# Flamingo layer, fold at the start: values folded straight to keys on the partitions, 13 of 77 keys by transposes, one mixed order of value and key units

## What is computed

```python
x = x + tanh(g_xattn[0]) * xattn(layernorm(x), ctx_768, Wq, Wk, Wv, Wo, bo)   # softmax over 77 keys, 16 heads
x = x + tanh(g_ffn[0]) * (layernorm(x) @ W[idx] + b[idx])                     # idx = argmax(log_softmax(logits) - log(-log(u)))
```

## Time and profile before

| | us |
|---|---|
| median of 3 runs (1070.23 to 1073.98) | 1071.11 |
| the profiled execution | 1072.84 |
| its span, first to last instruction | 1070.8 |
| PE busy in it | 1049.6 |
| DVE busy in it | 931.8 |
| mean granted clock of PE | 0.998 |

### The profile page before, as it was taken

How to read it: one execution, slowest core, us unless ns; L and a number is a source line. 1 busy time by engine, 2 the same in 40 slices (tenths; PEclk the granted TensorE clock), 3 DMA queues, 4 the chain that set the end, 5 groups by cost and what they waited for, 6 DMA issues and landing times.

```text
span 1070.8 us, 16059 instructions
## 1 busy us (share of the span) xinstructions
PE 1049.6 (98%) x5369; PEld 531.6 (50%) x5369; DVE 931.8 (87%) x1397; ACT 347.6 (32%) x549; POOL 304.6 (28%) x444
## 2 busy tenths in 40 slices
PE   8888999999999999999999999999999999999998
PEld 6554444444554455544554455444554455445443
DVE  4878798899888988899889988899889988898895
ACT  3685332223232323223222323223222323232331
POOL 0663422212222222212222222212221222222221
PEclk9999999999999999999999999999999999999999
DMA  8799555555555454545555454545454554545453
GB/s 308 158 186 177 128 114 109 118 109 112 114 111 120 100 124 104 125 102 119 108 117 113 108 118 107 127 96 125 105 120 106 114 113 112 117 103 123 105 99 93
DMA packets 366602, 130.30 MB, mean 122 GB/s; under 512 B 345152, under 2 KB 346228, under 8 KB 366580
## 3 DMA queue, kind: packets, MB, share of 16 engines
q1 hardware_dynamic: 366084, 129.22, 56.0%
q10 hardware_dynamic: 432, 0.79, 0.4%
q0 software_dynamic: 64, 0.00, 0.0%
HBM read 27.21 MB, written 16.78 MB: 41 GB/s over the span
## 4 chain that ended last, share of the span: by engine, by line
PE 87%; DMA 4%; DVE 4%; SPq 3%; ACT 1%; POOL 1%; issue 1%; DVEq 0%; ACTq 0%
PE banks L1092 82%; SPq L440 3%; PE banks L1297 3%; DMA late<-late 2%; PE banks L1131 1%; DVE red L807 1%; DMA pick_area<-in_L_ffn_u 1%; PE banks L1198 1%; DVE late L376 1%; DMA vw_area<-last_slot 0%; DMA last_slot<-late 0%; POOL last_slot L565 0%; DVE last_slot L1019 0%; DVE fold_area L883 0%; DVE early L836 0%
## 5 line engine op out<-in xcount | busy, mean ns | idle before, releaser
L1092 PE MATMUL banks<-fold_area,early 128*128 128x462 f16 (+1 forms) x2304 | 410.6, 336 | 0.3 <-DMA early<-early 0.3
L1092 PE MATMUL banks<-vw_area,late 128*128 128x512 f16 x1701 | 379.1, 380 | 5.6 <-DMA late<-late 5.6
L1092 PEld LDWEIGHTS banks<-fold_area,early 128*128 128x128 f16 x2304 | 224.0, 97 | 187.6 <-DMA early<-early 0.8
L1092 PEld LDWEIGHTS banks<-vw_area,late 128*128 128x128 f16 x1701 | 166.4, 98 | 198.5 <-issue 6.7
L605 POOL TENSOR_TENSOR stats<-stats,cst 128x1 f32<-128x1 f32 x64 | 12.1, 189 | 650.1 <-DVE stats L1034 650.1
L973 DVE TENSOR_REDUCE stats<-banks 128x6 f32<-128x462 f32 (+1 forms) x192 | 111.6, 581 | 81.1 <-PE banks L1092 81.1
L1092 PE MATMUL banks<-late,last_slot 128*128 128x512 f16 x744 | 170.7, 379 | 0.4 <-DMA last_slot<-late 0.4
L783 ACT ACTIVATE late<-late 128x1232 f16<-128x1232 f32 (+1 forms) x66 | 79.1, 1199 | 208.1 <-DVE late L992 207.8
L733 ACT ACTIVATE late<-last_slot 128x512 f16<-128x512 f32 x64 | 40.3, 630 | 325.9 <-DVE last_slot L1046 325.9
L769 ACT ACTIVATE late<-late,cst 128x462 f32<-128x462 f32 (+1 forms) x192 | 120.7, 629 | 56.1 <-DVE late L979 56.1
L1092 PEld LDWEIGHTS banks<-late,last_slot 128*128 128x128 f16 x744 | 72.2, 97 | 89.0 <-DMA last_slot<-late 1.4
(11 more groups left out here) (115 smaller groups left out, 689.3 us busy)
## 6 DMA issues: line engine op xcount, KB each, us to landing
out<-last_slot SPq DMA_DIRECT2D x64, 256.0 KB, 2.2
early<-in_x SPq DMA_DIRECT2D x61, 256.0 KB, 2.7
fold_area<-in_L_xattn_Wo SPq DMA_DIRECT2D x4, 512.0 KB, 10.0
vw_area<-in_L_xattn_Wq SPq DMA_DIRECT2D x2, 1024.0 KB, 10.9
vw_area<-in_L_xattn_Wk SPq DMA_DIRECT2D x2, 768.0 KB, 12.4
late<-late SPq DMA_TRANSPOSE x66, 4.9
vw_area<-in_L_ffn_W SPq DMA_DIRECT2D x1, 1024.0 KB, 7.8
early<-early SPq DMA_TRANSPOSE x64, 3.1
```

Of the source, the lines that this page charges most:

```text
L1092: mm = nc.tensor.matmul(ps, lhs(l), rhs(r), start=first and n == 0, stop=last and n == 2)
```

## The change

Value units give the keys on the partitions directly. For a batch and a group of four heads (two pairs of heads; `FOURS` = 4), four matmuls of 64 contraction rows and 64 output rows write the first 64 keys of four heads, each with all 512 output columns: the row half is the head's half of the pair, the column half (partitions 0 to 63 or 64 to 127) is the pair. There are 16 such units of 1024 elements for each partition. The other 13 keys of each head (`REST`) are folded as before, transposed: four "remainders", one for each 128 output columns, with 16 matmuls of 52 columns (4 batches x 13). ACT copies their 832 elements in two instructions, POOL splits them, and one DMA transpose of 2048 columns for each turns them: 4 in place of 16.

One list, `VISITS`, gives the order to all engines. Four PSUM pairs are visited in the old ring order. The first projection now stands before the spread of Wo. Four of 16 value units are staged (5, 8, 11, 14). The query copies move from ACT to DVE. All transposing of Wq is done before the first key unit, which waits for it. From value unit 10 on there are four key units to one value unit, and eight key units at the end. Since the memory is laid out anew, FFN weights are loaded once. On SP the loads of x for batches 1 to 3 (ACT issued them before) stand behind the last value unit, around the transpose of x for tile 0; `bias` follows.

Probabilities are laid out to match: for each of 16 heads 64 keys in chunks 0 to 7, then 16 times 13 in chunks 8 and 9. ACT's high part and DVE's low part are two instructions each (1024 and 208 elements), and `EARLY` becomes 6.

```diff
+    CORE = DH
+    REST = J - CORE
+    MAIN = HEADS * CORE // P
...
-        EARLY = BANKS[1][1] * J // P
+        EARLY = BANKS[1][1] * CORE // P
...
-        STAGED_VALUES = [0, 2, 4]
+        STAGED_VALUES = [5, 8, 11, 14]
         STAGED_KEYS = [1, 5]
-        PROJECTED_AFTER = [7, 10, 13]
-        SPREAD_AFTER = 17
-        TURNED_AFTER = 22
-        KEYS_TURNED_AFTER = [1, 5, 9]
...
+        PROJECT, REMAINDER, VALUE, SPREAD, TURN, KEY = range(6)
+        VISITS = [(PROJECT, 0), (PROJECT, 1), (REMAINDER, 0), (VALUE, 0), (REMAINDER, 1), (VALUE, 1), (PROJECT, 2), (REMAINDER, 2),
+                  (VALUE, 2), (REMAINDER, 3), (VALUE, 3), (PROJECT, 3), (VALUE, 4), (VALUE, 5), (SPREAD, 0), (VALUE, 6), (TURN, 0),
+                  (VALUE, 7), (TURN, 1), (VALUE, 8), (TURN, 2), (VALUE, 9), (TURN, 3)]
+        for n in range(10, VALUES):
+            VISITS += [(KEY, 4 * (n - 10) + m) for m in range(4)] + [(VALUE, n)]
+        VISITS += [(KEY, v) for v in range(UNITS - HP, UNITS)]
+
+        def pair_of(kind, n=0):
+            return ROUND[place_of(kind, n) % len(ROUND)]
...
-            return ([KT - 1, 0][v % 2], v // 2) if v < 2 * HP else (v // HP - 1, v % HP)
...
+            return (v // HP + 1) % KT, v % HP
...
-            for t in range(KT - 1):
-                turn_values(t)
-            sp.wait_ge(vwT_done, 2 * UNITS)
...
+            sp.wait_ge(pads_set, 1)
+            for t in range(KT):
+                sp.wait_ge(side_lo, 4 * (t + 1))
+                sp.dma_start_transpose(vw_side[:, t].rearrange("p b c n -> p (b c) n"),
+                                       sides[:, t].rearrange("p b n -> p (b n)")).then_inc(side_turned, 16)
+            sp.wait_ge(v_folded, 4 * VALUES)
+            sp.dma_start(xin[:, 1, :], x[1, 0:P, :]).then_inc(x_loaded[1], 16)
...
             turn_x(0, 0)
-            turn_values(KT - 1, 0, B // 2)
+            for r in range(2, B):
+                sp.dma_start(xin[:, r, :], x[r, 0:P, :]).then_inc(x_loaded[r], 16)
             turn_x(0, 1)
-            sp.wait_ge(vw_turned[KT - 1], 16 * B // 2)
+            sp.wait_ge(v_stage_lo, len(STAGED_VALUES))
...
+            def side_split(t):
+
+                value, side = side_stage[t % 2], sides[:, t]
+                pool.wait_ge(side_staged, 2 * (t + 1))
+                nc.gpsimd.tensor_copy(side[:, :, 0:P + TAIL], value).then_inc(side_hi, 1)
+                pool.wait_ge(side_hi, t + 1)
+                nc.gpsimd.tensor_tensor(side[:, :, 2 * P:3 * P], value[:, :, 0:P], side[:, :, 0:P], ALU.subtract).then_inc(side_lo, 1)
...
+            copy_k(0)
...
-                nc.scalar.activation(ps[:, h0 * J:h1 * J], probs[:, h0 * J:h1 * J], ACT.Copy,
+                values = by_head(probs[:, h0 * J:h1 * J])
+                nc.scalar.activation(by_core(ps[:, h0 * CORE:h1 * CORE]), values[:, :, 0:CORE], ACT.Copy,
+                                     scale=2.0 ** PROB_BITS).then_inc(p_hi, 1)
+                nc.scalar.activation(by_rest(ps[:, MAIN * P + h0 * REST:MAIN * P + h1 * REST]), values[:, :, CORE:J], ACT.Copy,
...
+            def copy_q(n):
+
+                first = pair_of(TURN, n)
+                dve.wait_ge(wqT_done, 2 * n + 2)
+                dve.wait_ge(scale_q_ready, 1)
+                nc.vector.tensor_scalar(wqT[:, 2 * n:2 * n + 2, :], banks[:, first:first + 2, :], scale_q, None, ALU.mult).then_inc(wqT_copied, 1)
+
...
-                    low(ps[:, LOW + h0 * J:LOW + h1 * J], probs[:, h0 * J:h1 * J], 2.0 ** PROB_BITS,
-                        ps[:, h0 * J:h1 * J]).then_inc(p_lo, 1)
+                    values = by_head(probs[:, h0 * J:h1 * J])
+                    hi, lo = ps[:, 0:LOW], ps[:, LOW:2 * LOW]
+                    dve.wait_ge(p_hi, 2 * pieces_done(q, b, piece))
+                    cols = slice(h0 * CORE, h1 * CORE)
+                    low(by_core(lo[:, cols]), values[:, :, 0:CORE], 2.0 ** PROB_BITS, by_core(hi[:, cols])).then_inc(p_lo, 1)
+                    cols = slice(MAIN * P + h0 * REST, MAIN * P + h1 * REST)
+                    low(by_rest(lo[:, cols]), values[:, :, CORE:J], 2.0 ** PROB_BITS, by_rest(hi[:, cols])).then_inc(p_lo, 1)
...
+            def remainder(t):
+
+                first = pair_of(REMAINDER, t)
+                for h in range(HP):
+                    for e in range(2):
+                        rows = slice(DH * e, DH * e + DH)
+                        place = banks[:, first + e, 0:B * HP * REST].rearrange("p (b h j) -> p b h j", b=B, h=HP)[:, :, h, :]
+                        last_keys = vT[rows, h, :].rearrange("p (b j) -> p b j", b=B)[:, :, CORE:J]
+                        mm = nc.tensor.matmul(place, wo_raw[rows, h, t * P:(t + 1) * P], last_keys, start=True, stop=True)
+                        if h == HP - 1:
+                            mm.then_inc(side_done, 1)
+
+            def value_unit(n):
+
+                b, four = n // FOURS, n % FOURS
+                first = pair_of(VALUE, n)
+                for a in range(2):
+                    for e in range(2):
+                        rows, h = slice(DH * e, DH * e + DH), 2 * four + a
+                        nc.tensor.matmul(banks[CORE * a:CORE * (a + 1), first + e, :], vT[rows, h, b * J:b * J + CORE], wo_raw[rows, h, :],
+                                         start=True, stop=True).then_inc(v_folded, 1)
+
+            def key_fold(v):
+
+                k, h = key_unit(v)
                 for e in range(2):
                     rows = slice(DH * e, DH * e + DH)
+                    nc.tensor.matmul(banks[:, pair_of(KEY, v) + e, 0:BJ], wqT[rows, h, k * P:(k + 1) * P], kT[rows, h, :],
+                                     start=True, stop=True).then_inc(a_done, 1)
...
+            for place, (kind, n) in enumerate(VISITS):
+                taken_before(place)
+                if kind == PROJECT:
+                    keys_of(2 * n)
+                    keys_of(2 * n + 1)
+                if (kind, n) == (PROJECT, 0):
+                    pe.wait_ge(v_copied, 2)
+                    spread(WO, 2)
+                    spread(VV, 3)
...
-                taken = max(v for v in range(UNITS) if key_bank(v) == n // 2 * 2)
-                needed = LAST_TURN + -(-BANKS[n][1] // 2) - 1
+                taken = max(v for v in range(UNITS) if pair_of(KEY, v) == n // 2 * 2)
+                needed = UNITS - HP + (3, 5, 7)[n]
```

More of the change, by code:

```diff
@@ L343, in key_staged, with place_of, staged, staged_before @@
+        assert sorted(n for kind, n in VISITS if kind == KEY) == list(range(UNITS))
+        def place_of(kind, n=0):
+            return VISITS.index((kind, n))
+        def pair_of(kind, n=0):
+            return ROUND[place_of(kind, n) % len(ROUND)]
+        def key_unit(v):
+            return (v // HP + 1) % KT, v % HP
+        def staged(n):
+            return n in STAGED_VALUES
+        def staged_before(n):
+            return sum(m < n for m in STAGED_VALUES)
         def key_staged(v):
@@ L579, in _ @@
-            for n in range(staged_before(UNITS)):
-                staged_value(n)
-                if n == 7:
+                nc.gpsimd.tensor_tensor(pair_of_heads(k, 1, h), value, pair_of_heads(k, 0, h), ALU.subtract).then_inc(k_stage_lo, 1)
+            for kind, n in VISITS:
+                if kind == REMAINDER:
+                    side_split(n)
+                if kind == VALUE and staged(n):
+                    value_split(n)
+                if kind == KEY and key_staged(n):
+                    key_split(n)
+                if (kind, n) == (VALUE, 8):
@@ L582, in _ @@
                     x_scale(0, 0)
-            for n in range(key_staged_before(UNITS)):
-                staged_key(n)
-                if n == 1:
+                if (kind, n) == (KEY, 26):
                     x_scale(0, 1)
@@ L701, in _, with side_copied @@
-            act.dma_start(xin[:, 1, :], x[1, 0:P, :]).then_inc(x_loaded[1], 16)
-            for v in range(UNITS):
+            def side_copied(t):
+                act.wait_ge(side_done, 2 * (t + 1))
+                if t >= 2:
+                    act.wait_ge(side_lo, 4 * (t - 1))
+                for e in range(2):
+                    place = side_stage[t % 2].rearrange("p b (i e m) -> p b i e m", i=FOURS, e=2)[:, :, :, e, :]
+                    value = banks[:, pair_of(REMAINDER, t) + e, 0:B * HP * REST].rearrange("p (b i m) -> p b i m", b=B, i=FOURS)
+                    nc.scalar.copy(place, value).then_inc(side_staged, 1)
@@ new lines, in value_high @@
+            def value_high(n):
+                first = pair_of(VALUE, n)
+                act.wait_ge(v_folded, 4 * (n + 1))
+                if staged(n):
+                    m = staged_before(n)
+                    if m == 1:
+                        act.wait_ge(side_lo, 4 * KT)
+                    if m >= 2:
+                        act.wait_ge(v_stage_lo, m - 1)
+                    nc.scalar.copy(v_stage[m % 2], banks[:, first:first + 2, :]).then_inc(v_staged, 1)
+                else:
+                    if n >= VALUES - FOURS:
```

(32 more changed lines are left out.)

504 lines of the change are left out of this document (186 added, 318 removed).

## The result

The changed kernel took 1081.45 us (median of 6 runs, 1078.44 to 1083.81) against 1072.38 for the kernel before on the same chip: a ratio of 1.0084, 95% interval 1.0063 to 1.0106, so 9.1 us slower, where +4.7 was forecast. That is outside the forecast's own range (1074.4 to 1079) and inside the stated one (1066.0 to 1083.0). The profiled execution took 1080.38 with a span of 1078.4.

The account below looks back on a forecast made before the run. PE bounds the tiles, so the fold's start moves everything: 7.8 later first scores, minus 2.1 and 1.7 won before and in tile 0's attention, plus 0.7 for splits, +4.7: 1075.8 us median, range 1066.0 to 1083.0 (own 1074.4 to 1079).

Parts of the forecast that it names:

- The start: Fold up to the last projection: PE-bound, scaling of vT 2.9 us late at 28.5, projections ending at 48.75.
- Rival 3: Value units: the four 64x64 matmuls run as two pairs, 0.86 longer each; +13.2, 1084.3 us; chance 0.08.
- The middle: From the last projection on, DVE works without a gap; first key unit on PE at 63.25, for 61 before.
- The mixed groups: Four key units and a value: hand-over through bank pairs costs 4.36 us, not 3.3; two groups with one staged value 8.1.
- S: Start of the first scores on PE: forecast 95.7 for 87.86 before, 7.8 us late.
- The wait for the last key unit: Ahead of the first scores: the last key unit shares their bank pair, so they wait for DVE's very last low half.
- A: Start of the attention of tile 0: forecast 15.45 behind the first scores for 17.58 before, 2.1 us won.
- From A to the end: Attention of tile 0 onward: full clock wins 1.7 us, split probabilities lose 0.7, nothing lost in steady tiles.
- loss of 0.25 in each of three tiles: Three tiles without slack ahead of PE: the split probabilities cost 0.25 each, 0.7 us lost.
- Rival 4: Steady tiles: the probability split breaks the 0.74 us slack; about 1084 us at 0.9; chance 0.03.
- Rival 1: Fold: DVE's 13.3 us idle stays, with about 50 of work from 29.8; +2.1, 1073.2 us, no change; chance 0.28.
- Rival 2: Fold: the drain becomes the bound and the hand-over hides; first scores at 86, -5, 1066.1 us, faster; chance 0.19.

Follow-up runs that it names:

- a: Changed kernel with the spread of Wo again ahead of the projection of keys; ratio 1.0073 to the kernel before.
- g: Changed kernel with value unit 5 not staged through POOL, DVE taking its low parts; ratio 1.0067 to the kernel before.
- c: Changed kernel with the four scaled query copies back on ACT; ratio 1.0074 to the kernel before.
- e: Changed kernel with small PE transposes filling two gaps, 16 ahead of the first key unit and 14 ahead of the first scores; ratio 1.0061 to the kernel before.
- b: Changed kernel with the ring of bank pairs turned, so the last key unit avoids the first scores' banks; ratio 1.0045 to the kernel before.
- i: Changed kernel with a to d together and tile 0's high and low parts of x three key units later; 1069.78 us for 1072.87 before.
- j: Version i with value unit 5 also not staged through POOL; 1067.46 us for 1073.20 of the kernel before.
- h: Changed kernel with the split of each group's 64-key probabilities doubled on ACT and DVE; ratio 1.0096 to the kernel before.
- d: Changed kernel with value units 10 to 15 ahead of all key units; ratio 1.0036 to the kernel before.

## Why the prediction was right in direction and short by half

**The start held.** Scaling of vT was forecast at 28.5 and stood at 28.26; a value unit 1.0, measured 1.02; a remainder 1.85, measured 1.93; the end of the last projection 48.75, measured 48.66. Rival 3 is refuted by the records. PE idled 1.72 ahead of the second spread. The sum contained that wait, as it put the spread at 27.15 (measured 26.91) and the next projection at 27.45 (27.07); what it didn't say is that the wait could be had back (a).

**The middle was short by 1.6**, of which 1.3 is the product of the scales (1.72 for the 0.40 that the 2.3 of the powers contained). Value 5's staging on POOL was booked at no cost, since it is buffered; its cost is that DVE waits for it. The net cost is smaller: without the staging DVE has a low half more, and the first key unit gains 0.43 (g). The DVE prices taken from the rows held: 1024 elements 1.19 to 1.23, a query copy 1.28, following at 1.19.

**The mixed groups were right, their first one was not.** From value 12 to 13 DVE's low halves lie 4.28 apart (79.05, 83.33), forecast 4.36; from 13 to 15, with a staged one, 7.99 (91.32), forecast 8.1. But from the first key unit to the end of value 10 (PE's restart behind its low half, 72.34) I had 6.05 and the trace has 7.5. In versions a, c, e and g, at full clock, it is 7.15 to 7.2, so the lower clock adds 0.3. The 1.1 that is left I put down to the normalization of x for tile 0, which stands in no sum of mine: DVE does it between those key units (0.87 at 65.96 in the trace of g), ACT stands 1.08 until it has it, and the next key units' high parts come behind. No run takes it out alone. The last eight key units took 6.3 for 5.8, which wasn't followed. Together S came 3.25 later than forecast: 1.6 + 1.1 + 0.3 + 0.5, less 0.25 in the groups.

**The wait for the last key unit was right and incomplete.** The forecast had the first scores behind DVE's very last low half because of the bank pair, and b shows it. It didn't follow the gap to its second price: PE stands 2.79 us, and the scores then run at the lower clock, 1.7 us (e). The prediction said that this loss would vanish, as the gap ahead of attention shrinks; that came true there (attention 5.99), and the same 1.7 came back in the scores. Here a step of the sum failed: a won clock was booked without asking where the new gap lies. A stood 16.95 behind S for 15.45, the difference being this. It is 1.5 us of the miss; the 3.25 of S, most of it the product of the scales and the normalization of x, is the larger part.

**From A to the end** the forecast had 1.7 won and 0.7 lost; the profiled executions have 2.9 won. 1.66 is the attention's clock; 0.7 are waits of PE, which come to 4.1 before and 3.4 in the changed trace; two of before, 0.37 at 173.67 and 0.29 at 198.09, have one of 0.18 in their place. The rest is spread and wasn't followed. The forecast loss of 0.25 in each of three tiles doesn't show: PE idles 0.29 ahead of the last scores in both. So the profiled spans differ by only 7.6 us, the medians by 9.1. The six executions of the changed kernel say where to look for the difference: 1078.44 us with a mean clock of 1.000, 1079.26 and 1080.38 with 0.997, 1082.52 and 1082.78 with 0.995, 1083.81 with 0.994. The slower ones had more of the lower clock than the profiled one (1080.38); in which stretch, no trace shows.

**Luck in the total.** In the spans the forecast missed S by 3.25 and the way from S to A by 1.5, both too early, and the rest by 1.9 the other way (2.9 won for 1.0). The direction rests on what was shown, the late start and the mixed order; that +4.7 came as near as it did owes something to errors of opposite sign. And 1081.45 is nearer to the 1084 of rivals 3 and 4, which the traces refute, than to the forecast's 1075.8.

**Rivals.** Rival 1 took the waste as fixed. Busy time by windows, sum of 26.85 to 98.95 us of the changed kernel (columns as in the earlier trace rows):

```profile
sum 72.10, PE 60.46 PEld 33.08 DVE 56.23 ACT 43.44 POOL 43.70; mean PE 30.23 PEld 16.54 DVE 28.12 ACT 21.72 POOL 21.85
```

DVE worked 56.2 of 72.1 us and stood 15.9, for 13.3 before. From 29.80, where rival 1 begins its sum, it worked 53.9 and stood 15.2, for the 50 and 13.3 of that rival: it fails by the work (3.9) more than by the waste (1.9). Rival 2 (the hand-over hides) wasn't what this change does, but it is what the fold does once the order is another: i and j have PE's streams of key units with gaps of 0.3 to 0.6 and S at 67.4 and 66.0 from T0, where the rival's 86 would be 64.2. Rival 4 is refuted: the change leaves 0.55 of the slack of 0.74, and even the doubled split 0.39.

## What to carry to other kernels

A change that touches the order of a start-up brings small waits of its own (here 1.9, 2.8, 2.8 and 4.6 us of the first scores for a spread, a bank pair, an engine and a mixed order); undone one at a time they tell what each is worth, and here the three behind the start nearly added up when undone together, to a kernel faster than both. The first did not: it waits for two engines, and which of them is last changes from execution to execution. In a ring of buffers, mixing two kinds of units can make each hand-over cost its full latency (here 4.28 us a group for 3.3 of work); runs of one kind, the one that the next stage doesn't wait for first, let it hide. When a gap of an engine whose clock falls moves, move its clock loss with it in the sum: fill the gap or place it before work that something else bounds.

## What the runs showed of the hardware that was not expected

- DVE's product of two scales, one element a partition, took 1.71 to 1.73 us in all eight versions that stage value 5 (the change, a to e, h, i), each time begun inside POOL's subtraction of 2.12 to 2.13 that reads SBUF and ended with it, and 0.16 without it (g, j). Before, it took 0.40 and ended at 51.14, as POOL's copy of 0.70 from 50.42 did. The reciprocal at 53.15, with one input of one element, ran in 0.16 beside the same subtraction. The Trainium skill (SBUF — State Buffer, section SBUF: two separate sides) says that a VectorE instruction with two inputs in SBUF and a GpSimd instruction that reads SBUF exclude each other for the whole instruction. The trace agrees: the product has two inputs in SBUF. That a form with one input would go through at this place was not tried.
- One input does not always go through. DVE's normalization of x for tile 0 (`TENSOR_SCALAR` 128x512 f32, SBUF to SBUF) took 0.54 before, begun at 57.03 ahead of POOL's copy, which then took 0.91 for its usual 0.70. Begun inside a POOL instruction it took 0.87 in the changed kernel (67.12, POOL from 67.01 to 67.71) and 1.24 in d (70.75, POOL from 69.58 to 71.71), and ended 0.28 behind POOL both times.
- PE's clock fell behind gaps of 2.6 to 2.8 us ahead of the scores in the profiled execution of all six versions that had one (14.3 to 15.6 us for 72 matmuls, 12.67 and 12.84 without), and behind a gap of 2.56 ahead of the key units in three of five. It is not certain in every execution: one of the change and one of g (1077.01 us) have a mean clock of 1.000.
- Four 64x64 f32 matmuls of 512 columns, on four quarters of the array, took 1.02 us, and 0.92 to 0.94 each in a row of six (5.50 to 5.61 for 48 records).
